# Moving the one-hot rows of a batch between the third and the fourth sum on VectorE, in the merged loop of a graph and attention layer

## What is computed

```
xn = layernorm(x)
h = xn @ W_src                                     # 4 heads of 64
e = leaky_relu(a_src[src] + a_dst[dst])            # one logit for each edge and head
p = exp(e - segment_max(e, dst)[dst])
out = segment_sum(p / denom * h[src], dst)         # the graph branch; then a layernorm and PReLU
mix = linear_attention_and_mlp(xn)                 # the mixer branch, two layernorms in it
x = x + out + mix
x = x + experts(layernorm(x))                      # 8 experts, three products each
```

## Time and profile before

| | |
|---|---|
| median of 3 runs | 4765.23 us (4764.68 to 4774.9) |
| profiled execution | 4775.0 us, span 4773.2 us |
| TensorE matmul busy | 4267.7 us, 89% |
| VectorE busy | 3908.7 us, 82% |
| ScalarE busy | 2264.6 us, 47% |
| GpSimd busy | 1813.6 us, 38% |
| granted TensorE clock, mean | 0.944 |

### The profile page before, as it was taken

The page is one execution under the profiler, slowest core; times in us unless marked ns, Lnnn a source line. Parts: engine busy times, 40 slices in busy tenths (PEclk is TensorE's granted clock), DMA queues, the critical chain, the costliest instruction groups (busy, mean ns, idle before and its releaser), DMA issues. The chain is left out here.

```text
span 4773.2 us, 85825 instructions
## 1 busy us (share of the span) xinstructions
PE 4267.7 (89%) x22703; PEld 3319.2 (70%) x22704; DVE 3908.7 (82%) x10182; ACT 2264.6 (47%) x4194; POOL 1813.6 (38%) x1677
## 2 busy tenths in 40 slices
PE   8994888888888888888888885999999999999999
PEld 5663566666666656666666553788888888888888
DVE  7765888888888899888988986877778778778776
ACT  3331343343333343333333432666666666666666
POOL 0007777777777677776776750000000000000000
PEclk9996999998999899999998987999999999999999
DMA  5444766766666667666766663100000000000000
GB/s 189 152 135 138 202 194 202 210 197 190 198 209 199 191 195 216 200 197 187 217 204 191 195 184 110 38 28 15 28 28 14 28 22 21 28 15 28 28 15 19
DMA packets 440121, 603.08 MB, mean 126 GB/s; under 512 B 41544, under 2 KB 366672, under 8 KB 439888
## 3 DMA queue, kind: packets, MB, share of 16 engines
q1 hardware_dynamic: 360016, 378.46, 25.0%
q0 software_dynamic: 79872, 221.62, 17.3%
HBM read 312.66 MB, written 287.25 MB: 126 GB/s over the span
## 5 line engine op out<-in xcount | busy, mean ns | idle before, releaser
L817 POOL DMA_INDIRECT acc<-h_tab,strips x1664 | 1810.6, 1088 | 1028.5 <-issue 830.3
L1316 PE MATMUL ps<-acc 128*128 128x260 f32 x3328 | 991.9, 427 | 48.3 <-DVE acc L936 29.1
L951 DVE SCALAR_TENSOR_TENSOR acc<-acc,strips,ps 128x260 f32<-128x260 f32 x1664 | 796.5, 479 | 231.2 <-PE ps L1316 144.0
L1316 PEld LDWEIGHTS ps<-acc 128*128 128x128 f32 x3328 | 634.5, 208 | 195.5 <-issue 102.2
L936 DVE TENSOR_TENSOR acc<-acc 128x512 f32<-128x512 f32 x832 | 564.3, 683 | 0.0
L1818 ACT ACTIVATE exp<-ps,bn 128x512 f32<-128x512 f32 (+1 forms) x400 | 310.2, 776 | 510.9 <-PE ps L1885 507.3
L1135 ACT ACTIVATE strips<-ps 128x512 bf16<-128x512 bf16 x416 | 247.5, 595 | 428.7 <-PE ps L1292 424.7
L1883 PE MATMUL ps<-w_hi,b_hi 128*128 128x256 f32 x1568 | 444.9, 284 | 1.2 <-DVE exp L1722 1.2
L1885 PE MATMUL ps<-w_hi,b_lo 128*128 128x256 f32 x1568 | 443.6, 283 | 0.0
L1884 PE MATMUL ps<-w_lo,b_hi 128*128 128x256 f32 x1568 | 443.6, 283 | 0.0
L1730 DVE TENSOR_TENSOR a_lo<-exp,a_hi 128x512 fp32r<-128x512 f32 (+1 forms) x400 | 262.0, 680 | 183.4 <-ACT a_hi L1820 169.8
(11 more groups left out here) (256 smaller groups left out, 8116.7 us busy)
## 6 DMA issues: line engine op xcount, KB each, us to landing
side_tab<-acc SPq DMA_DIRECT2D x416, 520.0 KB
acc<-h_tab,strips POOLq DMA_INDIRECT x1664
strips<-xnt_tab SPq DMA_DIRECT2D x50, 512.0 KB
h_tab<-acc SPq DMA_DIRECT2D x25, 520.0 KB, 6.6
exp<-side_tab SPq DMA_DIRECT2D x100, 130.0 KB, 2.3
acc<-in_x SPq DMA_DIRECT2D x25, 512.0 KB, 5.3
base_tab<-acc SPq DMA_DIRECT2D x25, 512.0 KB, 3.2
xnt_tab<-acc SPq DMA_DIRECT2D x25, 512.0 KB, 6.0
```

The costliest lines, as they stand in the source:

```text
L817: pool.indirect_dma_start(G[s][:, b * GU + u], None, h_tab, bass.IndirectOffsetOnAxis(REC[s][:, b * GU + u, 0:1], 0)).then_inc(g_in[s], 16)
L951: nc.vector.scalar_tensor_tensor(A[:, (b % 2) * GU + u], A[:, (k - 1) % (2 * GU) if k else 2 * GU], smt[s][:, k:k + 1], ps[u][:, 0:MW], AL ...
L1316: nc.tensor.matmul(ps[u][:, 0:MW], S32[b % 2][:, u], G[s][:, b * GU + u], start=True, stop=True).then_inc(g_mm.sem, 1)
```

## The change

The `onehot` of the batch moves behind the third sum, for all eight batches of a turn, with `relative` in front of it in b = 6. With it `mix_between`, the third sum and `mix_after` come one place earlier. No instruction is added or removed, and no other engine's order changes.

```diff
                             if b == GQ - 1:
                                 shrink(q, sq)
                                 message(q, sq, 0, 0)
                                 message(q, sq, 0, 1)
-                            if b < GQ - 2:
-                                onehot(dve, q, sq, b + 2)
+                        if here:
+                            mix_between(n, s * GQ + b)
+                            add(g, s, b, 2)
+                            mix_after(n, s * GQ + b)
+                        if ahead and b < GQ - 2:
+                            onehot(dve, q, sq, b + 2)
                         if q2 is not None:
                             if b == GQ - 2:
                                 relative(dve, q2, 1 - sq)
                                 onehot(dve, q2, 1 - sq, 0)
                             if b == GQ - 1:
                                 onehot(dve, q2, 1 - sq, 1)
                         if here:
-                            mix_between(n, s * GQ + b)
-                            add(g, s, b, 2)
-                            mix_after(n, s * GQ + b)
                             add(g, s, b, 3)
```

## The result

The changed kernel takes 4739.07 us (median of 5, 4738.37 to 4748.33), the kernel before 4766.3 (median of 5, 4764.68 to 4774.9). The ratio is 0.9944, 95% interval 0.993 to 0.9958: faster by 0.56%, 27 us. The forecast was 4761 with a range from 4742 to 4788.

The account below looks back on a forecast made before the run. Neither VectorE nor TensorE alone was taken as the bound; the path changes engine. Slot terms ended near -0.19 us a round, taken as 0.15, times 25: -4 us from 4765, giving 4761 us, range 4742 to 4788.

Parts of the forecast that it names:

- The two prices: Per slot: -0.18 us where VectorE doesn't wait, +0.42 us where it waits for the third sum's product.
- the fifth rival: Dependent neighbours cost nothing extra, so no saving and 0.60 behind a wait; 15 us slower, 4780; chance 0.05.
- Slot 10's deviations: Slot 10: the one-hot no longer stands in front of the mixer's deviations on VectorE, -0.60 us.
- The new wait in slot 14: Slot 14: TensorE's transposes are held 1.28 us for slot 13's later one-hot.
- VectorE's 0.54 is lost here: Slots 13 to 1: VectorE gains 0.18 in 13, 14 and 15, but TensorE reaches slot 1's first product later, at -0.03.
- the hold of 1.28: Slot 14: TensorE waits 1.28 us for slot 13's one-hot, delaying the large products of slots 14 and 15.
- four waits of TensorE: Slots 14 to 1: TensorE's waits for VectorE, 0.24, 0.22, 0.42 and 0.43, together swallow 1.31 us of delay.
- the 0.18 of slot 6: Slot 6: the parted pair of sums saves 0.18 us, bringing the round to -0.19.
- the first rival: VectorE's saving survives if slot 13's late one-hot is hidden: -0.58 us a round, 14.5 us, 4751; chance 0.17.
- what is absorbed: Of the +0.42 at waiting third sums, later waits take back 0.12 after slot 12 and 0.40 after slot 2.
- The second rival: Fewer low-clock stretches around slots 5 to 8 if VectorE arrives earlier; some 20 us faster, 4742; chance 0.11.
- The fourth rival: Low clock falls on slots 13 to 15 because of the new hole there; 45 us slower, 4806; chance 0.09.

Follow-up runs that it names:

- dev_only: Kernel before, with the one-hot moved only in slots 10 and 13, behind the mixer's deviations but ahead of the third sum: 4718.91 us, ratio 0.9914.
- after_c: The changed kernel itself, run again on the chip where the kernel before takes 4762.6 us: 4746.61 us, ratio 0.9958.
- keep_10_13: Changed kernel, but in slots 10 and 13 the one-hot stands ahead of the deviations as before: ratio 1.0069 where before takes 5222.98 us.
- pairs_only: Kernel before, with the one-hot between third and fourth sum in slots 0, 1, 6, 7, 11, 14, 15 alone: ratio 0.9996 (before 5225.51 us).
- mix_only: Changed kernel, but in all 16 slots the one-hot stands behind the mixer's work and ahead of the third sum: ratio 0.9966 (before 5222.98 us).

## Why the prediction was wrong

**Right in kind and size.**
- The two prices. Sum, one-hot, sum is 1.00 us in the rows above, and slot 14, where nothing else is in play, shrinks from 7.84 to 7.65: 0.19 for the predicted 0.18. In after it does so in 20 of 24 rounds; in 4 it lasts 9.15, with low clock in it. That rules out the fifth rival, in which neighbours are free. The Trainium skill, "VectorE: DVE Perf Modes", section "The DRAIN you can't avoid", read as a rule that a dependent neighbour costs nothing more, is spoken against by these 0.19 us.
- Slot 10's deviations: -0.60 predicted, 6.63 to 5.80 = -0.83 measured. The rest is mostly the short row L158, which took 0.43 us before and 0.17 now. As an order effect alone dev_only puts the step at -0.57 a round.
- The new wait in slot 14: 1.28 predicted, 1.10 measured.
- The waits grow where it was said: slot 12 1.63 to 2.78, slot 9 0.73 to 0.91.

**The step that failed first: "VectorE's 0.54 is lost here".** The prediction set the hold of 1.28 against four waits of TensorE, 1.31 in all, and let TensorE reach slot 1 at -0.03. The waits were worth more than their idle rows: with the hold, TensorE's way through slots 14 and 15 is 1.54 us shorter, not 0.88 (0.24 + 0.22 + 0.42, all it could swallow before slot 0). So VectorE is the path from slot 13 to slot 1. Averaged over the rounds these slots last 31.54 us in before and 30.43 in after_c, 1.1 us less, where the step let nothing of VectorE's gain through. All parted pairs together are worth 1.03 us a round, not the 0.18 of slot 6. The prediction had also counted only the pairs of slots 13, 14 and 15 there; those of slots 0 and 1 stand in the same stretch, and the first rival's 0.58 left them out as well. This is the first rival's mechanism, to which 0.17 was given. I had the evidence against my step in the earlier trace rows: four waits for VectorE on the way of an engine mean that VectorE leads.

**The second step: what is absorbed.** The prediction charged slots 9, 12 and 2 with 0.42 each and took 0.12 and 0.40 of it back, as absorbed. With the one-hot back in front of these three sums the round is 1.15 us shorter (1.06 to 1.29 by the spread of the clock's price); three times 0.42 is 1.26. So little was absorbed. Slot 2 shows it without the clock: the prediction had it 0.02 longer, and it is 0.50 longer on average (5.10 to 5.60). That "its product or the transfer out of its buffer is late" was a guess on one row, and it hid 0.40 of a price of 0.42.

These two errors have opposite signs. Predicted: -0.60 for the deviations, -0.18 for slot 6, +0.74 for the waits and -0.15 where TensorE takes over the path (from +0.12 to -0.03), which is -0.19 and was taken as -0.15. Measured by the kernels beside each other: -0.57 - 1.03 + 1.15 = -0.45, and -0.59 in the first comparison.

**The clock.** The second rival was worth 20 us at 0.11. By the price above it came true with 16: the low clock of the loop fell from 395 to 361 us. Not in the way told, though. In slots 7 and 8 it fell from 3.7 to 2.4 us a round and in slot 6 from 1.6 to 1.1, as said; it also fell in slot 11 (5.4 to 4.8) and rose in slots 12 and 14 (0.6 to 1.5, 0 to 0.6). The fourth rival, slots 13 to 15, is there in small.

**The range.** The rivals were taken as alternatives, each with a time of its own. But an order that makes VectorE earlier also shifts the clock, and the two came together: 15 + 16 = 31 us against 14.5 or 20 alone. 4765 - 31 = 4734, near the 4739.07 measured and below a range that ended at the rival of 20 us.

**What isn't settled.** That there is a part of each is measured (slots 13 to 1 are shorter, the loop has 34 us less low clock); which change of a slot makes the clock fall or stay isn't. Dev_only has 95 us less low clock than before and after_c only 20 less, and I can't derive either from the idle rows. The split of the gain rests on the price of 0.48, which is a slope between rounds: no run changed the clock and nothing else.

## What to carry to other kernels

Where an engine full of work has several small waits for the same other engine, look whether that other one has any idle time in the stretch. Here it had none over 0.23 us, so it was the path, and the waits gave back more than their idle rows when the first engine was delayed. Place a movable instruction slot by slot: between two dependent instructions where the engine never waits, in front of the wait where it does; the uniform rule of this change gave 0.4 to 0.6%, the slot-wise one 1.25%, both where before takes some 4765 us; on the chips where it takes over 5100 us neither could be told from before. And where two traces differ in the granted clock, compare slots of full clock, for the sum of the times mixes both.

## What the hardware showed that I hadn't expected

- Moving an instruction changes how long short ones at fixed places take. L158 in slot 10 took 0.43 us before, and 0.17 now. It takes 0.17 in keep_10_13 and pairs_only too, whose slot 10 has the order of before, so it isn't the one-hot in front of it; the cause is open. Slot 15 lost 0.34 us (6.47 to 6.13) where the parted pair explains 0.18. The other 0.17 is behind the fourth sum: L928, which needs that sum, starts 0.67 us after it in before, dev_only and mix_only and 0.50 after it in every kernel with the pair of slot 15 parted. Why is open as well.
- Chips of one kind differ by 8 to 10% on the same program (4763 us against 5138 to 5226), with waits of up to 9 us that the trace puts down to "remote" (late results of TensorE in the place shown above), and about twice the time at the low clock. A difference of half a per cent has to be repeated on a second chip: it was 0.56% and 0.42% in the two comparisons where before takes some 4765 us, and 0.16% and 0.04%, neither clear of nothing, on two of the other chips.
- TensorE filled with extra products in one slot had its full clock there and less in the next ones (0.1 us instead of 1.9 in slot 7, 4.1 instead of 2.7 in slot 9).
